# Loading the second batch's keys and queries one block earlier in a two-layer cross-attention kernel

## The reference

```python
h = _layernorm(x, gamma, beta)
Q = (h @ Wq).reshape(B, NQ, 16, 64)
K = (context @ Wk).reshape(B, NC, 16, 64)
V = (context @ Wv).reshape(B, NC, 16, 64)
attn = softmax(einsum('bihd,bjhd->bhij', Q, K), axis=-1) * scale
vals = einsum('bhij,bjhd->bihd', attn, V).reshape(B, NQ, INNER)
return x + vals @ Wo + bo
```

## Time and profile before

| | before |
|---|---|
| runs, us | 1124.32, 1126.2, 1128.36 |
| median, us | 1126.2 |
| span of the profiled execution, us | 1126.9 |
| TensorE busy, share of the span | 93% |
| VectorE, ScalarE, GpSimd busy | 67%, 51%, 35% |
| mean granted TensorE clock | 0.958 |

### The profile page before, as it was taken

How to read it: one execution, slowest core, us unless ns; L and a number is a source line. 1 busy time by engine, 2 the same in 40 slices (tenths; PEclk the granted TensorE clock), 3 DMA queues, 4 the chain that set the end, 5 groups by cost and what they waited for, 6 DMA issues and landing times. The chain is left out here.

```text
span 1126.9 us, 31634 instructions
## 1 busy us (share of the span) xinstructions
PE 1046.1 (93%) x12060; PEld 741.3 (66%) x12060; DVE 759.8 (67%) x1409; ACT 574.5 (51%) x1139; POOL 389.9 (35%) x273
## 2 busy tenths in 40 slices
PE   4977899999999998979596999999999999999997
PEld 2552566666666665655433777777777777777786
DVE  3646777888788878520575677667767777767652
ACT  2533567777677676642243444544444344444442
POOL 4822012111211112111102554545545555555542
PEclk8977889999999999979898999999999999999998
DMA  3501434344544443030002111111111110111100
GB/s 106 138 2 53 143 117 140 121 130 141 143 131 128 129 142 106 2 97 1 1 22 57 52 55 40 40 53 55 53 55 43 45 53 23 52 53 55 34 4 3
DMA packets 48462, 79.41 MB, mean 70 GB/s; under 512 B 8803, under 2 KB 35253, under 8 KB 48405
## 3 DMA queue, kind: packets, MB, share of 16 engines
q1 hardware_dynamic: 48404, 78.61, 23.1%
HBM read 51.13 MB, written 21.96 MB: 65 GB/s over the span
## 5 line engine op out<-in xcount | busy, mean ns | idle before, releaser
L1374 ACT ACTIVATE P<-PS 125x448 f32<-125x448 f32 x384 | 206.7, 543 | 270.7 <-PE PS L1283 268.7
L1264 POOL TENSOR_TENSOR Pl<-P 125x896 f16<-125x896 f32 x128 | 229.9, 1801 | 242.3 <-ACT P L1374 242.3
L1012 DVE TENSOR_REDUCE m<-PS 128x1 f32<-128x500 f32 x336 | 220.6, 674 | 120.2 <-PE PS L1003 118.4
L918 DVE TENSOR_REDUCE m_part<-PS 128x1 f32<-128x500 f32 x336 | 212.6, 674 | 59.6 <-PE PS L821 58.3
L896 ACT ACTIVATE Pb<-PS 125x448 f32<-125x448 f32 x384 | 187.9, 545 | 36.8 <-PE PS L796 36.1
L1299 PE MATMUL PS<-cNh,P 125*128 125x97 f16 x1344 | 198.1, 208 | 0.1
L1301 PE MATMUL PS<-cNh,Pl 125*128 125x97 f16 x1344 | 197.4, 207 | 0.0
L1300 PE MATMUL PS<-cNl,P 125*128 125x96 f16 x1344 | 196.9, 206 | 0.0
L1300 PEld LDWEIGHTS PS<-cNl,P 125*128 125x128 bf16 x1344 | 131.9, 98 | 25.5 <-issue 0.2
L1299 PEld LDWEIGHTS PS<-cNh,P 125*128 125x128 bf16 x1344 | 131.2, 98 | 15.8 <-issue 3.2
L1281 PE MATMUL PS<-Qh,cTh 110*125 110x448 f16 x384 | 139.0, 362 | 1.3 <-DVE Qh L1450 1.3
(11 more groups left out here) (170 smaller groups left out, 1555.5 us busy)
## 6 DMA issues: line engine op xcount, KB each, us to landing
Kst<-k_halves SPq DMA_DIRECT2D x144, 125.0 KB, 2.7
k_halves<-KH SPq DMA_DIRECT2D x16, 750.0 KB, 3.3
cx<-in_ctx SPq DMA_DIRECT2D x16, 562.5 KB
d_cx<-in_ctx SPq DMA_DIRECT2D x16, 562.5 KB
c_halves<-cHi SPq DMA_DIRECT2D x16, 281.2 KB, 2.7
c_halves<-cLo SPq DMA_DIRECT2D x16, 281.2 KB, 3.0
cTh<-c_halves SPq DMA_DIRECT2D x16, 281.2 KB, 2.9
cTl<-c_halves SPq DMA_DIRECT2D x16, 281.2 KB, 3.6
```

The costliest lines, as they stand in the source:

```text
L918: nc.vector.tensor_reduce(m_part[:, t, part:part + 1], PS[:, 6 + k % 2, 0:SP], AX.X, ALU.max).then_inc(s_reduced, 1)
L1012: nc.vector.tensor_reduce(m21[:, t, part:part + 1], PS[:, S1[k % 2], 0:SP], AX.X, ALU.max).then_inc(n_red, 1)
L1264: nc.gpsimd.tensor_tensor(Pl[:, c % NP], P1[:, c % NP], high, ALU.subtract).then_inc(n_low_p, 1)
L1374: nc.scalar.activation(P1[:, c % NP, half * HALF:(half + 1) * HALF], PS[0:KC, u % 3, 0:HALF], ACT.Exp).then_inc(n_exp, 1)
```

## The change

`load_halves` gets a flag that leaves out its wait for the slot to be free. The preceding block calls it twice more, for batch 1, right behind batch 0's calls. The loop block's body leaves out the two calls for batch 1 (i = 0, par = 0). Everything else stays.

```diff
-        def load_halves(sp, i, par, half, queries_made=None):
+        def load_halves(sp, i, par, half, queries_made=None, ahead=False):
...
-            if half == 0:
+            if half == 0 and not ahead:
                 wait_for(sp, n_st, (n - 1) * 2 * NC)
...
                 load_halves(sp, -1, 1, 0, g_high)
                 load_halves(sp, -1, 1, 1, g_low)
+                load_halves(sp, 0, 0, 0, ahead=True)
+                load_halves(sp, 0, 0, 1, ahead=True)
...
                 def body(i, par):
-                    if inside(i, par, 0) and inside(i, par, 1):
+                    if inside(i, par, 0) and inside(i, par, 1) and not (isinstance(i, int) and i == 0 and par == 0):
                         load_halves(sp, i, par, 0)
                         load_halves(sp, i, par, 1)
```

## The result

| | before | after |
|---|---|---|
| runs, us | 1124.32 to 1128.66 (5) | 1120.45 to 1123.19 (5) |
| median, us | 1128.36 | 1122.08 |
| span of the profiled execution, us | 1126.9 | 1120.3 |
| mean granted TensorE clock | 0.958 | 0.961 |

The change makes the kernel faster: the ratio of the runs is 0.996 with a 95% interval of 0.9946 to 0.9974, which is 2.9 to 6.1 us. The forecast was 1121.1 us. The medians lie 6.3 us apart, because the two later executions of the kernel before came out high (1128.66 and 1128.57); over the 14 to 24 executions of it beside the experiments its median was 1125.9 to 1126.2, which is where the forecast started.

What follows compares the result with a forecast made beforehand. TensorE, busy 93% of the span, was taken to bound the kernel. 3.83 us from the removed wait and 1.25 from the clock give 5.1, so median 1126.2 becomes 1121.1 us; whole range 1118.7 to 1124.0.

Steps and rivals of the forecast that it cites:

- The hole: Loop block's start: TensorE's wait for batch 1's `Qh`, 606.42 to 610.25, goes: -3.83 us.
- The clock's share: Loop's start: the clock rises 4.81 us after the first score, so less work runs at half speed: -1.25 us.
- The sum: Whole kernel: 3.83 + 1.25 = 5.1 us gained, median 1126.2 to 1121.1 us, 0.45% less.
- Late rise: Rival, loop's start: the clock rises 7.5 us after the restart, gain only 3.8 us, 1122.4 us; chance 0.14.
- no fall: Rival, loop's start: the clock never falls, gain 7.0 us, 1119.2 us; chance 0.06.
- The rise after 7.5 us, read as 5.1 by the rule on transposes: Preceding block's restart: transposes don't count toward full clock, so 7.5 us shrink to 5.1, near 4.81.
- Another wait: Rival, loop's chunk 3: ScalarE's copy of a late `d_cx` replaces the removed wait; gain 3.1 us or none; chance 0.13.
- Slower: Rival, preceding block: new transfers delay batch 0's `Qh` by 5.8 us; +2.7 us in sum, 1128.9 us; chance 0.06.
- The row of 8.21 us: Loop block: `Qh` took 8.21 us to land, two transfers ahead and two behind; alone it keeps the slower case possible.
- the ring-order rule: DMA queue: each engine takes one queue's descriptors in ring order, so a later transfer delays nothing, price 0.

Runs made afterwards that it cites:

- experiment 1: The kernel before, with batch 1's four loads kept in the loop block but issued ahead of batch 1's `d_cx`: 1121.28 us, ratio 0.9956.
- experiment 2: The changed kernel, with `d_cx` of batch 1 also issued in the preceding block, behind batch 1's keys and queries: 1121.68 us, ratio 0.9959.
- experiment 3: The changed kernel, with only batch 1's high halves issued ahead and its low halves back in the loop block: 1121.19 us, ratio 0.9952.
- experiment 4: The changed kernel, with `d_cx` of batch 1 issued in the preceding block directly ahead of batch 0's `Qh`: 1128.14 us, ratio 1.0022.

## Why the prediction was right, point by point

- **The hole.** 3.83 us were to go, with 16 us of cover. The piece at 605.54 has no idle time ahead of it, and the same holds with the loads in the loop block (experiment 1), with `d_cx` away (2) and with half of the loads (3).
- **The clock's share.** 1.25 us were forecast and 1.00 measured. The step that was off is the stretch of low clock: the forecast kept its start at 1.0 us after the first score and ended it 4.81 us after that score. It began before the score and ended 4.29 us after it, so the low work was 4.29 us against a forecast 3.80. That the sizes are so near is partly luck, as this moves from execution to execution, with the same instructions of TensorE at the loop's start. First score to first values was 10.90 us before, of which the hole was 3.83, so 7.07 remain. It was 5.8 us in experiments 1 and 4, where the clock gives 1.3 us. It was 7.2 in experiments 2 and 3 (609.12 - 601.91 and 609.05 - 601.87) and in the kernels with 55 and 65 added matmuls, where the clock gives nothing at this place. With the clock held it was 4.08 and 4.09 us.
- **Where the clock's share went in experiments 2 and 3.** Their medians are as good as that of experiment 1. What the loop's start lost there, the preceding block had won: behind TensorE's restart at L623 the granted clock rose after 4.8 and 4.7 us, against 7.6 in experiment 1, 7.9 in the changed kernel and 7.5 before. This table counts from that restart, in us:

| | restart to first score | first score to first values | sum |
|---|---|---|---|
| before | 44.14 | 10.90 | 55.04 |
| changed | 44.56 | 6.20 | 50.76 |
| experiment 1 | 44.20 | 5.76 | 49.96 |
| experiment 2 | 42.79 | 7.21 | 50.00 |
| experiment 3 | 42.71 | 7.18 | 49.89 |

- **The sum.** 5.1 us were forecast, 4.84 found at the place of the change, and 2.9 to 6.1 by the runs. By the table it is 4.3 us in the profiled execution of the changed kernel and 5.0 to 5.2 in experiments 1 to 3.
- **Late rise, no fall.** The low stretch after the first score was never absent without added matmuls. In experiments 2 and 3 it ended about 6.4 us after that score, and the loop's start won the hole alone, as the late rise had it. The time of the whole kernel didn't follow, as the table shows.
- **The rise after 7.5 us, read as 5.1 by the rule on transposes.** With the same turns ahead, the rise came 4.7 to 7.9 us after the restart in these five executions. Less the 2.45 us of the turns that is 2.2 to 5.4. So neither 7.5 nor 5.1 is a fixed delay, and that 5.1 lay near 4.81 was chance.
- **Another wait.** It doesn't occur: experiment 2 takes the one candidate away and wins nothing.
- **Slower.** Batch 0's `Qh` landed in 2.4 us as before, so the new transfers behind it held nothing up. One reason that the forecast gave doesn't hold by its own rows: the last issue ends at 579.50 and `Qh` lands at 580.0, so it had not landed before the new issues begin. In the changed kernel the first of them starts at 577.55 and `Qh` lands at 575.61 + 2.4 = 578.0. The forecast's price for it being late, 1128.9 us, was met by experiment 4 at 1128.14. What makes such a transfer late is one ahead of it, not one behind. The row of 8.21 us alone could not tell these apart; the ring-order rule that the prediction set beside it was right here. The price was met in sum and not in its parts: the step from the issue of batch 0's `Qh` to the first score is 606.85 - 573.95 = 32.90 us in experiment 4 and 602.16 - 575.61 = 26.55 in the changed kernel, 6.35 us more where 5.8 + 2.0 = 7.8 were forecast.
- **What the prediction left unsaid.** It took the removed wait as a matter of when the loads are issued. Experiment 1 shows that the place behind `d_cx` on the queue was the whole of it, and a swap of two calls would have done.

The version with 9 added matmuls has the lowest median, 1119.13 us. Its trace is 2.1 us shorter at the loop's start than the change's, but the intervals of the two ratios overlap, so that the runs alone don't separate them.

## What to carry to other kernels

A transfer that is late at the start of a stage should first be looked for on its queue: what is ahead of it, how large that is, and who needs that. Swapping two issues cost nothing here and gave the same 0.4% as moving four of them a block earlier. A stall of TensorE costs more than its length, as the work behind it ran at 1.2 GHz for 4.0 us in experiment 4, 4.81 in the kernel before and 7.5 behind L623. And where code is added ahead of a long loop, the packets on the instruction queue are the row to compare, since 28 instructions more cost 36 and 40 us.

## What the runs showed of the hardware that was not expected

- TensorE's loop of 1640 instructions (105 KB) runs without fetches from iteration to iteration when it touches 7 blocks of 256 instructions, and stands still for 5 to 6 us in each of 5 iterations when it touches 8: 85 packets instead of 40, and medians of 1158.5 to 1169.4 us instead of 1119 to 1122. The same loop fits or doesn't by where it starts.
- `Qh`, 168 KB, landed in 2.4 to 2.8 us with nothing large ahead, and in 8.2 and 8.8 us behind `d_cx` (562.5 KB from 125 partitions). At the changed kernel's loop start `d_cx` is the only transfer but for one 16 KB packet of instructions, and from 602.16 to 605.54 us the DMA share is 0.32 at 130 GB/s (windows above). The Trainium skill ("DMA: Bandwidth & Descriptors", the section on why a DMA increments its semaphore by 16) says that a transfer is split over the largest number up to 16 that divides the partitions, which is 5 of 16 (0.31) for 125. The trace agrees. It also explains why `Qh` behind it is late: in experiment 4 eleven of its sixteen counts are there after 2.5 us and the last five only behind those of `d_cx`. That they belong to the same five engines is inferred from the equal numbers and the order in time, as no row names an engine. No run here took another partition count.
